# Two residual convolutions on one core: the work behind each of the last three 5x5 halves shared by three engines

## The chip, the cores and the metric

The kernel runs on one core of one Trainium2 chip. The metric is the device time of the core in microseconds (us), the median of three timed executions; a separate profiled execution gives the trace.

## The reference

`x` is 16 images of 32 channels, 128x128, float32. Two blocks follow each other, each with a group norm over 16 groups of two channels and a residual sum:

```python
x = x + conv3x3(gn(x), w3 * mask)      # padding 1; mask from a threshold on the mean |w3|
x = x + conv5x5(gn(x), w5) + bias      # written in the reference as a product of FFTs, padding 2
```

The 5x5 convolution is a circular convolution on a padded image, cut back to 128x128, so it equals a direct 5x5 convolution with padding 2.

## The kernel before

**Tiling.** An image is worked in two halves, so there are `HALVES` = 32 halves. The 128 partitions are four bands of 32 channels. TensorE multiplies 32x32 tiles of weights with 32 x 512 pieces of the image, sixteen of them for one tap (`tap`, L705), into four PSUM banks (`BANKS` = 4): banks 0 to 3 for the 3x3, banks 4 to 7 (`X5_BANK`) for the 5x5 convolution. The four banks of the 5x5 are used by every half anew; there is no second set.

**Precision.** Images and weights are split in a high and a low float16 part. A 5x5 half is three passes of 25 taps: the high image with the high weights, the high image with the low weights (both from the one tile `s5`, into which ScalarE copies `s5_hi` and `s5_lo` in turn, `weights5`, L363), and the low image `x5_lo` with `s5_hi` (`low_image`, L765). Tap 0 of the first two passes stands apart (`first5`, `last5`). The next half's first pass (`first5`) starts with `start=True` over the same banks, so it waits for `a5_go`, which ScalarE raises when it has evicted all four.

**Order.** The loop over steps `s` runs conv3x3 of half `s` and conv5x5 of half `s - LAG` with `LAG` = 3. Steps 3 to 31 mix both. In steps 32, 33 and 34 only the 5x5 convolution of halves 29, 30 and 31 is left: these are called lone steps here. There is no planner; the order on each engine is that of its program, and semaphores tie the engines together.

**Behind a half.** When `b5_whole` says that a half's matmuls are done, ScalarE evicts its four banks to `conv_out` (`take_conv5`, L350, activation at L355), GpSimd adds each to `mid` in place (`add_out`, L318, L322), and SP stores `mid` to the output with four DMAs of 256 KB, one for each band of partitions (L277), once all four additions are done. SP's program ends with waits on `out_stored` (L289). `mid` has five slots, `conv_out` one: an eviction of bank `b` waits for the addition of bank `b` of the half before.

**On VectorE.** In a step it computes the low image (`low5`, L574, L580), and for the next half the group statistics (`group_stats`, L526; `scale_of`, L541), the normalization (`normalize5`, L609, L557) and the clearing of padding rows (L565). ScalarE then makes the high image from it (`high5`, L343, L348). The order in a step is at L660 to L698 for VectorE and L382 to L426 for ScalarE; `low3` (L572) and `take_conv3` (L592) are its 3x3 work.

Of the kernel before, what the change touches and what calls it, by code (L numbers as in the profile page):

```python
# [48 lines left out]
def two_blocks(nc, x, w3_dram, thr_dram, w5_dram, bias_dram, mix_dram, out):  # L49
# [7 lines left out]
    with ExitStack() as ctx:  # L57
# [3 lines left out]
        def sem(name):  # L61
            return ctx.enter_context(nc.semaphore(name))
# [101 lines left out]
        var_ready = sem("var_ready")  # L164
        gstep = sem("gstep")
        out_added = sem("out_added")

        def has3(s):
            return 0 <= s < HALVES
# [11 lines left out]

        def exchange_number(s):
            return 1 if s == 2 else s // 2 + 1

        def column(kind):
            return slice(0, 1) if kind == "x" else slice(1, 2)
# [5 lines left out]
        def quad(q):  # L192
            return slice(q * C, (q + 1) * C)
# [16 lines left out]
        @block.sync  # L210
        def _(sp):
            def load_own(h):
                for j in range(Q):
                    sp.dma_start(x_own[quad(j), h % X_SLOTS, :, :], own_rows(x[h // 2], h % 2, j),
                                 ).then_inc(x_own_in[h % X_SLOTS], 16)

            def load_bands(h):
                for i in range(Q):
                    y0, y1, at = band(h % 2, i, 1)
                    sp.dma_start(x_bands[quad(i), h % XB_SLOTS, at:at + y1 - y0, :], x[h // 2][:, y0:y1, :],  # L220
                                 ).then_inc(x_bands_in[h % XB_SLOTS], 16)

            def move_rows(h, i, j, k, to, rows, at):

                sp.dma_start(mid_bands[quad(to), k % MB_SLOTS, at:at + rows.stop - rows.start, :],  # L225
                             mid[quad(j), h % MID_SLOTS, i, :].rearrange("p (a w) -> p a w", a=A)[:, rows, :],
                             ).then_inc(mid_bands_in[k % MB_SLOTS], 16)

            def move_mid(h):
                sp.wait_ge(mid_made, PIECES * (h + 1))  # L230
                for i in range(Q):
                    for j in range(Q):
                        move_rows(h, i, j, h, i, slice(0, A), 2 + A * j)

            def move_edges(n):

                for i in range(Q):
                    move_rows(2 * n + 1, i, 0, 2 * n, i, slice(0, 2), 2 + A * Q)
                    if i + 1 < Q:
                        move_rows(2 * n + 1, i, Q - 1, 2 * n, i + 1, slice(A - 2, A), 0)  # L240
                for i in range(Q):
                    move_rows(2 * n, i, Q - 1, 2 * n + 1, i, slice(A - 2, A), 0)
                    if i:
                        move_rows(2 * n, i, 0, 2 * n + 1, i - 1, slice(0, 2), 2 + A * Q)

            for q in range(Q):
                sp.dma_start(w3[quad(q), :, :], w3_dram.rearrange("i a b o -> i (a b) o")).then_inc(w3_loaded, 16)
            sp.dma_start(thr[:, :], thr_dram.rearrange("(a o) -> a o", a=1).to_broadcast([P, 1])).then_inc(w3_loaded, 16)
            load_bands(0)
            load_bands(1)  # L250
            sp.dma_start(mix[:, :], mix_dram).then_inc(mix_loaded, 16)
            load_bands(2)
            load_bands(3)
            load_own(0)
            for q in range(Q):
                sp.dma_start(w5[quad(q), :, :], w5_dram.rearrange("i a b o -> i (a b) o")).then_inc(w_loaded, 16)
                sp.dma_start(bias[quad(q), :], bias_dram.rearrange("(o a) -> o a", a=1)).then_inc(w_loaded, 16)
            load_own(1)
            load_bands(4)
            move_mid(0)  # L260
            load_own(2)
            move_mid(1)
            move_edges(0)
            load_bands(5)
            load_bands(6)
            load_own(3)
            move_mid(2)
            load_bands(7)
            load_own(4)
            load_bands(8)  # L270

            for s in range(LAG, STEPS + 1):
                if has5(s - 1):
                    k = s - 1 - LAG
                    sp.wait_ge(out_added, BANKS * (k + 1))
                    for j in range(Q):
                        sp.dma_start(own_rows(out[k // 2], k % 2, j), mid[quad(j), k % MID_SLOTS, :, :],  # L277
                                     ).then_inc(out_stored[k % MID_SLOTS], 16)
                if has3(s + XB_SLOTS):
                    sp.wait_ge(norm1, s + 2)  # L280
                    load_bands(s + XB_SLOTS)
                if has3(s):
                    move_mid(s)
                    if s % 2:
                        move_edges(s // 2)
                    if has3(s + X_SLOTS):
                        load_own(s + X_SLOTS)
            for n in range(MID_SLOTS):
                sp.wait_ge(out_stored[n], 16 * Q * len(range(n, HALVES, MID_SLOTS)))  # L289

        @block.gpsimd
        def _(pool):
# [24 lines left out]

            def add_out(k, b):  # L318

                pool.wait_ge(conv5_out, BANKS * k + b + 1)  # L320
                m = mid[:, k % MID_SLOTS, b, :]
                nc.gpsimd.tensor_tensor(m, m, conv_out[:, b, :], ALU.add).then_inc(out_added, 1)  # L322

            for k in range(HALVES):
                for b in range(BANKS):
                    add_out(k, b)

        @block.scalar
        def _(act):
# [20 lines left out]
            def take_conv5(k, b):  # L350

                act.wait_ge(b5_whole, k + 1)
                if k:
                    act.wait_ge(out_added, BANKS * (k - 1) + b + 1)
                nc.scalar.activation(conv_out[:, b, :], psum[:, X5_BANK + b, :], ACT.Identity,  # L355
                                     bias=bias[:, 0:1], scale=unscale[:, 1:2]).then_inc(conv5_out, 1)

# [24 lines left out]
            for s in range(STEPS + 1):  # L382
# [8 lines left out]
                if has3(s):  # L391
                    act.wait_ge(c3_inner, 3 * s + 1)
                    weights3(s3_lo, 1, 1)
                if has5(s - 1):
                    take_conv5(s - 1 - LAG, 2)
                    take_conv5(s - 1 - LAG, 3)
                if has5(s):
                    act.drain().then_inc(a5_go, 1)  # L398
                if has3(s):
# [5 lines left out]
                if has5(s):  # L405
                    if s == LAG:
                        act.wait_ge(w5_split, 3)
                    act.wait_ge(a5_inner, 2 * (s - LAG) + 1)
                    weights5(s5_lo)
                if gathered:  # L410
                    take_root(gathered[0])
                if s == 2:
# [16 lines left out]
        def _(dve):  # L429
# [179 lines left out]
            def normalize5(k):  # L609
# [3 lines left out]
                scalings += 1  # L613
                clear_pad(1, k, scalings)

            setup3()
            scalings = 0
            stats_in(0, range(BANKS))
# [41 lines left out]
            for s in range(LAG, STEPS):  # L660
                gathered = exchanged(s - 1)
                if s > HALVES:
                    dve.drain().then_inc(bank3_go, 1)
                low5(s - LAG)
                if has3(s):
                    low3(s)
                if s == LAG:
# [28 lines left out]
                    stats_in(s + 5, range(BANKS))  # L696
                if len(gathered) > 1:
                    scale_of(gathered[1])  # L698

        @block.tensor  # L700
        def _(pe):
# [212 lines left out]
```

## Time and profile before

| | |
|---|---|
| Timed executions | 880.46, 880.9 (median), 882.7 us |
| The profiled execution's own time | 882.4 us |
| Its span, first to last instruction | 880.6 us |
| TensorE matmul, busy | 789.2 us (90%) |
| VectorE, busy | 679.1 us (77%) |
| ScalarE, busy | 326.0 us (37%) |
| GpSimd, busy | 317.3 us (36%) |
| Mean granted TensorE clock | 0.964 |
| Chain that ended last | PE 77%, DVE 10%, issue 4%, SPq 3% |

[...] In a timeline, PE is TensorE's matmul, PEld its weight load, DVE VectorE, ACT ScalarE, POOL GpSimd; a letter q behind an engine is its queue (issues, waits and drains). What stands in square brackets is the idle time of the engine ahead of the row and what ended it. L711 is the line of the matmuls, L398 ScalarE's drain that raises `a5_go`.

### The profile page before, as it was taken

What the parts mean: (1) busy time and instruction counts of PE and PEld (TensorE: products, weight loads), DVE (VectorE), ACT (ScalarE), POOL (GpSimd) and SP (SyncE); (2) the same over time, 40 slices, a digit from 0 to 9 for tenths busy, and PEclk for the clock granted to TensorE, in tenths of its full rate; (3) what the DMA queues carried; (4) which work ended last, traced back from release to release, by engine and by line L of the source; (5) the groups of instructions that cost most, each with busy time, mean ns of one, the idle gap of its engine ahead of it and who ended that gap; (6) DMA issues with size and microseconds to landing.
All of it is one profiled execution on the core that took longest, in us unless ns stands there. A gap on an engine that the chain in (4) does not pass through costs nothing.

```text
span 880.6 us, 108990 instructions
## 1 busy us (share of the span) xinstructions
PE 789.2 (90%) x52300; PEld 705.5 (80%) x52300; DVE 679.1 (77%) x989; ACT 326.0 (37%) x417; POOL 317.3 (36%) x154
## 2 busy tenths in 40 slices
PE   1673579999999999999999999999999999998884
PEld 1552368888989889899888888988989889987773
DVE  5576378979898989989897989898998878664210
ACT  0122024344344444344434434444434443433331
POOL 1020004444433333334434444333334444443332
PEclk9887789999999999999999999999999999999998
DMA  8954965969787787868696868878795556454222
GB/s 178 211 120 116 221 153 135 234 144 225 172 215 201 198 207 188 218 168 223 151 236 144 221 178 206 211 196 208 182 220 157 158 147 160 107 136 114 66 56 56
DMA packets 83843, 150.52 MB, mean 171 GB/s; under 512 B 20960, under 2 KB 28384, under 8 KB 79712
## 3 DMA queue, kind: packets, MB, share of 16 engines
q1 hardware_dynamic: 79200, 145.92, 67.7%
q10 hardware_dynamic: 4608, 4.23, 1.9%
q14 instruction: 25, 0.20, 0.1%
q8 instruction: 10, 0.16, 0.1%
HBM read 75.60 MB, written 33.59 MB: 124 GB/s over the span
## 4 chain that ended last, share of the span: by engine, by line
PE 77%; DVE 10%; issue 4%; SPq 3%; DMA 2%; ACTq 1%; ACT 1%; DVEq 1%; POOL 0%; POOLq 0%
PE psum L711 76%; DVE x L572 3%; SPq L225 2%; DMA x_bands<-x_dram 2%; DVE bn_in L498 1%; DVE x_bands L557 1%; ACTq L398 1%; DVE bn_out L600 1%; DVE mid L592 1%; DVEq L595 1%; DVE mid_bands L557 1%; SPq L220 0%; DVE product L530 0%; POOL mid L322 0%; DVE deviation L534 0%
## 5 line engine op out<-in xcount | busy, mean ns | idle before, releaser
L322 POOL TENSOR_TENSOR mid<-mid,conv_out 128x512 f32<-128x512 f32 x128 | 308.0, 2437 | 502.4 <-ACT conv_out L355 489.1
L711 PE MATMUL psum<-x_hi,s 32*32 32x512 f16 x25600 | 378.0, 382 | 21.4 <-issue 9.7
L711 PEld LDWEIGHTS psum<-x_hi,s 32*32 32x32 f16 x25600 | 343.0, 88 | 47.3 <-issue 16.6
L711 PE MATMUL psum<-x,s 32*32 32x512 f16 x13824 | 228.9, 391 | 28.0 <-DVEq L595 14.7
L711 PEld LDWEIGHTS psum<-x,s 32*32 32x32 f16 x13824 | 176.4, 88 | 78.9 <-issue 49.2
L711 PE MATMUL psum<-x_lo,s_hi 32*32 32x512 f16 x12800 | 186.1, 376 | 3.5 <-issue 3.3
L711 PEld LDWEIGHTS psum<-x_lo,s_hi 32*32 32x32 f16 x12800 | 175.8, 88 | 8.4 <-issue 4.6
L580 DVE TENSOR_TENSOR x_lo<-mid_bands,x_hi 128x2560 f16<-128x2560 f32 x32 | 102.3, 3197 | 59.4 <-PE psum L711 59.0
L572 DVE TENSOR_TENSOR x<-x_bands,x 128x2304 f16<-128x2304 f32 x32 | 100.6, 3144 | 35.2 <-PE psum L711 35.2
L355 ACT ACTIVATE conv_out<-psum,bias,unscale 128x512 f32<-128x512 f32 x128 | 94.4, 769 | 60.1 <-PE psum L711 60.0
L364 ACT ACTIVATE s<-s_lo 128x800 f16<-128x800 f16 x32 | 27.9, 871 | 179.3 <-PE psum L711 179.3
L592 DVE SCALAR_TENSOR_TENSOR mid<-psum,unscale,x_own 128x1024 f32<-128x1024 f32 x64 | 79.1, 1277 | 8.1 <-PE psum L711 7.2
L341 ACT ACTIVATE x<-x_bands 128x2304 f16<-128x2304 f32 x32 | 67.9, 2122 | 45.8 <-DVE x_bands L565 22.9
L498 DVE BATCH_NORM_STATS2 bn_in<-x_bands 128x6 f32<-128x512 f32 x128 | 78.2, 673 | 3.2 <-DMA x_bands<-x_dram 3.1
L600 DVE BATCH_NORM_STATS2 bn_out<-mid 128x6 f32<-128x512 f32 x128 | 78.1, 668 | 2.3
L348 ACT ACTIVATE x_hi<-mid_bands 128x2560 f16<-128x2560 f32 x32 | 74.5, 2328 | 5.0 <-DVE mid_bands L565 5.0
L557 DVE TENSOR_SCALAR x_bands<-x_bands,gmean,gscale 128x2304 f32<-128x2304 f32 x32 | 71.2, 2226 | 0.1
L364 ACT ACTIVATE s<-s_hi 128x800 f16<-128x800 f16 x32 | 27.9, 872 | 113.6 <-PE psum L711 113.6
L557 DVE TENSOR_SCALAR mid_bands<-mid_bands,gmean,gscale 128x2560 f32<-128x2560 f32 x32 | 52.5, 1640 | 6.6 <-DMA mid_bands<-mid 4.5
L361 ACT ACTIVATE s<-s_lo 128x128 f16<-128x128 f16 x64 | 20.5, 321 | 40.5 <-PE psum L711 30.5
L334 ACT ACTIVATE root<-gvar 128x1 f32<-128x1 f32 x32 | 6.5, 202 | 71.6 <-DVE gvar L538 45.9
L530 DVE SCALAR_TENSOR_TENSOR product<-every_mv,mix 128x128 f32<-128x128 f32 x29 | 21.1, 726 | 15.4 <-DMA every_mv<-mv_scratch 15.0
(74 smaller groups left out, 175.1 us busy)
## 6 DMA issues: line engine op xcount, KB each, us to landing
x_own<-x_dram SPq DMA_DIRECT2D x128, 256.0 KB
mid_bands<-mid SPq DMA_DIRECT2D x512, 64.0 KB
out_dram<-mid SPq DMA_DIRECT2D x128, 256.0 KB
x_bands<-x_dram SPq DMA_DIRECT2D x96, 288.0 KB, 6.1
x_bands<-x_dram SPq DMA_DIRECT2D x32, 272.0 KB, 7.4
mid_bands<-mid SPq DMA_DIRECT2D x224, 32.0 KB
every_mv<-mv_scratch ACTq DMA_DIRECT2D x16, 256.0 KB
w<-L_conv_kernel_dram SPq DMA_DIRECT2D x4, 100.0 KB, 18.6
```

The source lines that it names most:

```text
L322: nc.gpsimd.tensor_tensor(m, m, conv_out[:, b, :], ALU.add).then_inc(out_added, 1)
L341: nc.scalar.activation(x3[:, :, 2:2 + W], x_bands[:, h % XB_SLOTS, :, :], ACT.Copy).then_inc(x3_go, 2)
L348: nc.scalar.activation(x5_hi[:, :, 2:2 + W], mid_bands[:, k % MB_SLOTS, :, :], ACT.Copy).then_inc(hi5_done, 1)
L355: nc.scalar.activation(conv_out[:, b, :], psum[:, X5_BANK + b, :], ACT.Identity, bias=bias[:, 0:1], scale=unscale[:, 1:2]).then_inc(conv5_ ...
L364: nc.scalar.activation(s5[:, :, :], source[:, :, :], ACT.Copy).then_inc(w5_go, 1)
L498: nc.vector.bn_stats(bn_in[:, h // 2 % 2, h % 2, b, :], rows.rearrange("p a w -> p (a w)")).then_inc(bn_x, 1)
L557: nc.vector.tensor_scalar(v, v, gmean[:, which:which + 1], gscale[:, which:which + 1], ALU.subtract, ALU.mult).then_inc(scaled, 1)
L572: nc.vector.tensor_tensor(at, x_bands[:, h % XB_SLOTS, :, :], at, ALU.subtract).then_inc(x3_go, 1)
L580: nc.vector.tensor_tensor(x5_lo[:, :, 2:2 + W], mid_bands[:, k % MB_SLOTS, :, :], x5_hi[:, :, 2:2 + W], ALU.subtract).then_inc(b5_go, 1)
L592: nc.vector.scalar_tensor_tensor(mid[:, h % MID_SLOTS, at, :], psum[:, X3_BANK + at.start:X3_BANK + at.stop, :], unscale[:, 0:1], x_own[:, ...
L600: nc.vector.bn_stats(bn_out[:, h % 2, b, :], mid[:, h % MID_SLOTS, b, :]).then_inc(bn_mid, 1)
L711: ins = nc.tensor.matmul(psum[quad(j), bank + i, :].rearrange("p (a w) -> p a w", a=A), w[quad(i), at, :], src[quad(i), A * j + dy:A * (j ...
```

## The change

Halves from `LATE` = 29 on are treated differently.

- **Eviction.** ScalarE evicts banks 0 and 1, VectorE banks 2 and 3 in one `tensor_scalar` instruction of 128x1024 (`take_late`). ScalarE waits for `late_out` before it raises `a5_go`.
- **Additions.** GpSimd adds banks 0 and 1, VectorE banks 2 and 3 in one `tensor_tensor` (`add_late`), for halves 29 and 30 in the next step behind the copy named below, for half 31 right behind its eviction.
- **Weight copy.** In steps 32, 33 and 34 the copy of `s5_lo` into `s5` is made by VectorE, behind `low5`. That of `s5_hi` stays with ScalarE.
- **Stores.** Each late half is stored in two groups of four DMAs of 128 KB: banks 2 and 3 when `late_added` has counted it, then banks 0 and 1 when GpSimd's two additions are counted.

`take_late(29)` and `take_late(30)` stand ahead of `low5` in steps 33 and 34. `added_before` gives the counts of evictions and additions, four for an early half and two for a late one.

```diff
--- before.py
+++ after.py
@@ -164,6 +164,8 @@
         var_ready = sem("var_ready")
         gstep = sem("gstep")
         out_added = sem("out_added")
+        late_out = sem("late_out")
+        late_added = sem("late_added")
 
         def has3(s):
             return 0 <= s < HALVES
@@ -181,6 +183,13 @@
 
         def exchange_number(s):
             return 1 if s == 2 else s // 2 + 1
+
+        LATE = HALVES - LAG
+        HALF_BANKS = BANKS // 2
+
+        def added_before(k, b):
+
+            return BANKS * min(k, LATE) + HALF_BANKS * max(k - LATE, 0) + b
 
         def column(kind):
             return slice(0, 1) if kind == "x" else slice(1, 2)
@@ -213,6 +222,11 @@
                 for j in range(Q):
                     sp.dma_start(x_own[quad(j), h % X_SLOTS, :, :], own_rows(x[h // 2], h % 2, j),
                                  ).then_inc(x_own_in[h % X_SLOTS], 16)
+
+            def store_out(k, banks):
+                for j in range(Q):
+                    sp.dma_start(own_rows(out[k // 2], k % 2, j)[:, banks, :], mid[quad(j), k % MID_SLOTS, banks, :],
+                                 ).then_inc(out_stored[k % MID_SLOTS], 16)
 
             def load_bands(h):
                 for i in range(Q):
@@ -272,10 +286,14 @@
             for s in range(LAG, STEPS + 1):
                 if has5(s - 1):
                     k = s - 1 - LAG
-                    sp.wait_ge(out_added, BANKS * (k + 1))
-                    for j in range(Q):
-                        sp.dma_start(own_rows(out[k // 2], k % 2, j), mid[quad(j), k % MID_SLOTS, :, :],
-                                     ).then_inc(out_stored[k % MID_SLOTS], 16)
+                    if k < LATE:
+                        sp.wait_ge(out_added, BANKS * (k + 1))
+                        store_out(k, slice(0, BANKS))
+                    else:
+                        sp.wait_ge(late_added, k - LATE + 1)
+                        store_out(k, slice(HALF_BANKS, BANKS))
+                        sp.wait_ge(out_added, added_before(k, HALF_BANKS))
+                        store_out(k, slice(0, HALF_BANKS))
                 if has3(s + XB_SLOTS):
                     sp.wait_ge(norm1, s + 2)
                     load_bands(s + XB_SLOTS)
@@ -286,7 +304,7 @@
                     if has3(s + X_SLOTS):
                         load_own(s + X_SLOTS)
             for n in range(MID_SLOTS):
-                sp.wait_ge(out_stored[n], 16 * Q * len(range(n, HALVES, MID_SLOTS)))
+                sp.wait_ge(out_stored[n], 16 * Q * sum(1 if k < LATE else 2 for k in range(n, HALVES, MID_SLOTS)))
 
         @block.gpsimd
         def _(pool):
@@ -317,12 +335,12 @@
 
             def add_out(k, b):
 
-                pool.wait_ge(conv5_out, BANKS * k + b + 1)
+                pool.wait_ge(conv5_out, added_before(k, b + 1))
                 m = mid[:, k % MID_SLOTS, b, :]
                 nc.gpsimd.tensor_tensor(m, m, conv_out[:, b, :], ALU.add).then_inc(out_added, 1)
 
             for k in range(HALVES):
-                for b in range(BANKS):
+                for b in range(BANKS if k < LATE else HALF_BANKS):
                     add_out(k, b)
 
         @block.scalar
@@ -351,7 +369,7 @@
 
                 act.wait_ge(b5_whole, k + 1)
                 if k:
-                    act.wait_ge(out_added, BANKS * (k - 1) + b + 1)
+                    act.wait_ge(out_added, added_before(k - 1, b + 1))
                 nc.scalar.activation(conv_out[:, b, :], psum[:, X5_BANK + b, :], ACT.Identity,
                                      bias=bias[:, 0:1], scale=unscale[:, 1:2]).then_inc(conv5_out, 1)
 
@@ -391,9 +409,11 @@
                 if has3(s):
                     act.wait_ge(c3_inner, 3 * s + 1)
                     weights3(s3_lo, 1, 1)
-                if has5(s - 1):
+                if has5(s - 1) and s - 1 < HALVES:
                     take_conv5(s - 1 - LAG, 2)
                     take_conv5(s - 1 - LAG, 3)
+                if s > HALVES:
+                    act.wait_ge(late_out, s - HALVES)
                 if has5(s):
                     act.drain().then_inc(a5_go, 1)
                 if has3(s):
@@ -405,8 +425,9 @@
                 if has5(s):
                     if s == LAG:
                         act.wait_ge(w5_split, 3)
-                    act.wait_ge(a5_inner, 2 * (s - LAG) + 1)
-                    weights5(s5_lo)
+                    if s < HALVES:
+                        act.wait_ge(a5_inner, 2 * (s - LAG) + 1)
+                        weights5(s5_lo)
                 if gathered:
                     take_root(gathered[0])
                 if s == 2:
@@ -612,6 +633,23 @@
                 normalize(1, k)
                 scalings += 1
                 clear_pad(1, k, scalings)
+
+            def take_late(k):
+
+                dve.wait_ge(b5_whole, k + 1)
+                if k == LATE:
+                    dve.wait_ge(out_added, BANKS * LATE)
+                else:
+                    dve.wait_ge(late_added, k - LATE)
+                at = slice(HALF_BANKS, BANKS)
+                nc.vector.tensor_scalar(conv_out[:, at, :], psum[:, X5_BANK + at.start:X5_BANK + at.stop, :],
+                                        unscale[:, 1:2], bias[:, 0:1], ALU.mult, ALU.add).then_inc(late_out, 1)
+
+            def add_late(k):
+
+                dve.wait_ge(late_out, k - LATE + 1)
+                m = mid[:, k % MID_SLOTS, HALF_BANKS:BANKS, :]
+                nc.vector.tensor_tensor(m, m, conv_out[:, HALF_BANKS:BANKS, :], ALU.add).then_inc(late_added, 1)
 
             setup3()
             scalings = 0
@@ -661,7 +699,13 @@
                 gathered = exchanged(s - 1)
                 if s > HALVES:
                     dve.drain().then_inc(bank3_go, 1)
+                    take_late(s - 1 - LAG)
                 low5(s - LAG)
+                if s >= HALVES:
+                    dve.wait_ge(a5_inner, 2 * (s - LAG) + 1)
+                    nc.vector.tensor_copy(s5[:, :, :], s5_lo[:, :, :]).then_inc(w5_go, 1)
+                if s > HALVES:
+                    add_late(s - 1 - LAG)
                 if has3(s):
                     low3(s)
                 if s == LAG:
@@ -696,6 +740,9 @@
                     stats_in(s + 5, range(BANKS))
                 if len(gathered) > 1:
                     scale_of(gathered[1])
+
+            take_late(HALVES - 1)
+            add_late(HALVES - 1)
 
         @block.tensor
         def _(pe):
```

## Rows read from the trace of the kernel before

**Rows 1.** Chain of waits that ended last, from 820 us: start us, us, what.
```profile
823.51 2.58 ACTq L398
...
826.13 7.41 PE psum L711 x393
...
833.56 0.88 ACT s L364
...
846.08 2.58 ACTq L398
...
868.02 0.79 ACT conv_out L355
...
868.88 2.48 POOL mid L322 x2
...
872.58 1.22 POOL mid L322
```
**Rows 2.** Timeline of TensorE, 802 to 870 us: start, duration, instruction, [idle before <- releaser].
```profile
826.13 7.38 PE L711 MATMUL psum<-x_hi,s 32*32 32x512 f16 x400 [2.94 <-ACTq L398]
834.49 5.79 PE L711 MATMUL psum<-x_hi,s 32*32 32x512 f16 x400 [0.98 <-ACT s L364]
...
848.70 6.99 PE L711 MATMUL psum<-x_hi,s 32*32 32x512 f16 x400 [2.93 <-ACTq L398]
```
**Rows 3.** Table by windows: length, busy (xcount) of PE, PEld, DVE, ACT, POOL; PEclk, DMA share, GB/s.
```profile
803.55:806.90 3.35, 3.35 (x128) 2.56 (x144) 0.09 (x2) 0.00 (x0) 3.35 (x3) 0.50 0.45 141
...
811.90:817.40 5.50, 5.50 (x400) 5.21 (x409) 2.68 (x7) 0.04 (x1) 0.00 (x0) 1.00 0.79 188
827.40:830.80 3.40, 3.40 (x155) 2.78 (x143) 1.53 (x2) 0.00 (x0) 3.40 (x2) 0.51 0.00 0
848.70:851.30 2.60, 2.60 (x112) 1.98 (x113) 0.05 (x1) 0.00 (x0) 2.60 (x3) 0.50 0.00 0
```
**Rows 4.** Groups by form, single lines and a stretch of the timeline: the durations of the operations.
```profile
L592 DVE SCALAR_TENSOR_TENSOR mid<-psum,unscale,x_own 128x1024 f32<-128x1024 f32 x64 | 79.1, 1277 | 8.1 <-PE psum L711 7.2
...
L465 DVE CAST s_hi<-w3n 128x256 f16<-128x256 f32 x1 | 0.3, 294 | 0.0
L467 DVE COPY s<-s_hi 128x128 f16<-128x128 f16 x1 | 0.2, 194 | 0.0
L470 DVE COPY s<-s_hi 128x160 f16<-128x160 f16 x1 | 0.2, 193 | 0.0
...
L355 ACT ACTIVATE conv_out<-psum,bias,unscale x16: 768/777/784, 800.7 to 870.0; 128x512 f32<-128x512 f32 x16
...
L364 ACT ACTIVATE s<-s_lo x3: 869/869/869, 811.0 to 855.7; 128x800 f16<-128x800 f16 x3
...
823.25 2.79 ACT L355 ACTIVATE conv_out<-psum,bias,unscale 128x512 f32<-128x512 f32 x4 [2.35 <-PE psum L711]
823.35 2.82 DVE L580 TENSOR_TENSOR x_lo<-mid_bands,x_hi 128x2560 f16<-128x2560 f32 x1 [8.42 <-PE psum L711]
```
**Rows 5.** Timeline of TensorE at its earlier holes, and the clock there by windows.
```profile
128.08 2.04 PE L711 MATMUL psum<-x_lo,s_hi 32*32 32x512 f16 x127 [1.71 <-issue]
131.72 1.52 PE L711 MATMUL psum<-x_lo,s_hi 32*32 32x512 f16 x90 [1.61 <-issue]
...
46.35 1.94 PE L711 MATMUL psum<-x,s 32*32 32x512 f16 x64 [2.10 <-DVEq L595]
...
46.20:49.20 3.00, 2.85 (x112) 2.27 (x124) 2.46 (x9) 0.51 (x2) 0.00 (x0) 0.50 0.27 66
126.30:128.10 1.80, 0.09 (x14) 0.02 (x7) 1.80 (x4) 0.67 (x1) 0.00 (x0) 1.00 0.30 73
130.20:131.70 1.50, 0.00 (x0) 0.00 (x0) 1.50 (x5) 0.00 (x0) 0.00 (x0) 1.00 0.35 83
```
**Rows 6.** Timeline of VectorE and ScalarE in the lone steps.
```profile
806.86 0.49 DVE L530 SCALAR_TENSOR_TENSOR product<-every_mv,mix 128x128 f32<-128x128 f32 x1 [3.26 <-DMA every_mv<-mv_scratch]
...
811.97 0.16 DVE L545 RECIPROCAL rinv<-root 128x1 f32<-128x1 f32 x1 [2.17 <-ACT root L334]
...
814.66 0.27 DVE L565 MEMSET mid_bands<- 32x256 f32 x1
...
841.15 2.32 ACT L348 ACTIVATE x_hi<-mid_bands 128x2560 f16<-128x2560 f32 x1
```
**Rows 7.** Timeline of GpSimd and VectorE, single instructions.
```profile
801.53 3.20 POOL L322 TENSOR_TENSOR mid<-mid,conv_out 128x512 f32<-128x512 f32 x1 [13.13 <-ACT conv_out L355]
804.69 1.27 POOL L322 TENSOR_TENSOR mid<-mid,conv_out 128x512 f32<-128x512 f32 x1
...
257.19 3.87 POOL L322 TENSOR_TENSOR mid<-mid,conv_out 128x512 f32<-128x512 f32 x1
...
259.85 3.63 DVE L572 TENSOR_TENSOR x<-x_bands,x 128x2304 f16<-128x2304 f32 x1
```
**Rows 8.** Timeline of SP's queue at single stores and one move, and the last transfer by window.
```profile
794.54 0.59 SPq L225 DMA_DIRECT2D mid_bands<-mid  x1
...
875.80 1.24 SPq L277 DMA_DIRECT2D out_dram<-mid  x1
...
874.90:879.90 5.00, 0.00 (x0) 0.00 (x0) 0.00 (x0) 0.00 (x0) 0.00 (x0) 0.50 0.87 210
```

## The prediction

> **What bounds the kernel now.** I read the chain of waits first, for the last 55 us, then the timeline of TensorE. The chain [rows 1] is TensorE's matmuls, broken in every lone 5x5 step (one with no 3x3 work) in two places and followed by a tail. The first break is 2.9 us: TensorE has finished a half (at 800.65, 823.23 and 845.80), four evictions run one after the other on ScalarE, and only the drain behind the last one lets the next half start (803.55, 826.13, 848.70). The second is 0.98 us, the copy of `s5_lo` into `s5` on ScalarE [rows 2]. In the tail the matmuls end at 868.0, GpSimd's fourth addition at 873.8, and the span 6.8 us later.
>
> The first break costs more than its length. [...] So the 400 matmuls behind the breaks take 7.38 and 6.99 us at 826.13 and 848.70, where an undisturbed pass takes 5.79 [rows 2]. Behind the 0.98 us break the clock stays at 1.00 [rows 3].
>
> **The first break.** Halves 29, 30 and 31 are late; half 28 is not, so the break at 800.65 stays whole. At the next two, ScalarE keeps banks 0 and 1, and VectorE takes banks 2 and 3 beside it in one 128x1024 instruction. ScalarE: an eviction takes 0.777 us and four take 2.79 [rows 4], a pitch of 0.67, so two take 1.45 and 1.35 us goes. VectorE: its first instruction behind the same release began 0.10 us after ScalarE's [rows 4]; the operation itself is not in the trace. It is bounded by 0.6 (twice as fast as the nearest) and 1.28; I take 1.28, since the 3x3 eviction L592 has the same shape, source and output type and one operand more [rows 4]. So it ends 1.38 us behind the release, a little before ScalarE's two. The added wait on `late_out` costs 0 to 0.2 us; I take 0.1. Behind it on ScalarE is queued the drain that releases TensorE. Each break shrinks by 1.25 us (bounds 1.0 to 1.35), two by 2.5, and 1.65 us of idle time stays in each.
>
> [...]
>
> **The clock behind the shorter break.** Does 1.65 us of idle time still let it fall? The nearest rows on one side are two holes of 1.71 and 1.61 us at 126 and 130 us, in which TensorE waited for nothing shown: the clock stayed at 1.00. On the other side a wait of 2.10 us ended at 46.35 and left the clock at 0.50 [rows 5]. I take "stays up". It returns 7.38-5.79 = 1.6 and 6.99-5.79 = 1.2 us, 2.8 together (bounds 0 and 2.8); I count 2.7.
>
> **The weight copies.** In the last three steps the copy of `s5_lo` moves to VectorE. ScalarE's takes 0.869 us [rows 4]. VectorE's float16 copies of 128 and 160 columns take 0.194 and 0.193 us, a cast of 256 from float32 0.294 [rows 4]. [...] I take 0.40. With VectorE's later start of 0.1 us the break goes from 0.98 to about 0.57: 0.4 us, 1.2 for three (bounds 0 to 1.6). VectorE is idle at those moments: its work ahead of them ends by 809.8, 829.0 and 848.8 [rows 6].
>
> That wait holds back what is queued on VectorE. In step 32 it is `group_stats`, `scale_of` and `normalize5(30)`, which ran from 806.86 to 814.93 [rows 6]. They start at about 811.3 and need 8.1 us less the 2.2 that they waited for the root behind ScalarE's copy, so they end near 817.4. `high5(30)`, which needs them, began at 818.57, behind ScalarE's other copy, and will want to begin at 818.2: hidden by 0.8 us, and by 3.1 until ScalarE is late for the next eviction (822.8, less 2.33 for `high5`); from there 1 us for each. In step 33 the copy and `add_late(29)` stand ahead of `normalize5(31)`, which moves from 826.10 to about 832 and ends by 834; its reader moves from 841.15 [rows 6] to 837.5. `low5` moves 1.3 us back and is wanted over 10 us later. All this at nothing.
>
> **Additions and stores.** In steps 33 and 34 VectorE adds behind the copy and SP stores later, in eight DMAs, with nothing else in SP's queue: nothing. Only the last half counts. ScalarE's first eviction frees GpSimd's first addition at 868.88, which ends at 870.14. VectorE's eviction ends at 869.4. Its addition then meets GpSimd's: an addition of 1.27 us took 3.20 when it started during VectorE's `low5`, and a `low3` begun at 259.85 took 3.63 us, of which the first 1.2 until GpSimd's addition ended at 261.06 [rows 7]. Each waits for the other's instruction. So VectorE's addition (1.15 by the shortest 128x1024 row, I take 1.2) runs from 870.1 to 871.3, and GpSimd's second to 872.5. SP's first store goes at 871.35 instead of 873.82. Stores of 256 KB were issued at a pitch near 0.65 us and moves of 64 KB take 0.59 [rows 8], so eight at 0.64: the last goes at 875.85, where it went at 875.80. Issue gains nothing; the transfer does. Four stores moved at 210 GB/s for 5.0 us, from 1.1 us behind the first issue, bound by transfer [rows 8]. Eight halves at 0.64 us ask for 205 GB/s and leave no backlog: the last lands at 875.85+1.1+0.65 = 877.6, and the span ends 0.7 us later, as before: 878.3, a gain of 2.3. I take 2.0, for the added wait between the groups. Bounds: 1.3, if the fourth store of each group holds SP for 1.24 us [rows 8], and 2.5, if the 1 MB simply starts 2.5 us earlier.
>
> [...]
>
> **Sum.** 2.5+2.7+1.2+2.0 = 8.4 us off the profiled execution, whose span is 880.6 and whose own time is 882.4, 1.5 over the median of the three runs, 880.9. The 1.8 us around the span stay. The executions differ by up to 2.2 us, about what one or two low stretches are worth, so the median may hold fewer of them than the profile; I don't correct for it. 880.9-8.4 = 872.5.
>
> **Rivals.**
> 1. The clock falls behind 1.65 us of idle time too. For it: the two holes are few, and 2.10 is not far. The 2.7 us stay away: 875.2.
> 2. VectorE at its upper bounds: copies as slow as ScalarE's, 880.9-7.2 = 873.7; or an eviction at twice its price, 2.6 us, which keeps both breaks and the falling clock, 880.9-3.2 = 877.7. Against both stand [rows 4].
> 3. A store costs by the piece, 5.0/4 = 1.25 us each whatever its size. Eight take 10 us from 872.5, the span ends at 883.2, a loss of 2.6 instead of a gain of 2.0: 877.1. Against it: 64 KB moves go out every 0.64 us without holding SP [rows 8].
> 4. Slower: VectorE's order turns against TensorE. The place is step 32, where the wait for `a5_inner` holds `normalize5(30)`. TensorE waits once `high5(30)` is 3.1 us late, 1 us for each; from 11.5 us on the kernel is slower, from 14 by over 0.3%; at 15 it is 884.4. Against it: the whole chain is 8.1 us, and nothing in it is new.
>
> **How the numbers follow.** Forecast 0.62; rival 1 0.21; rival 2 0.07, mostly the copies; rival 3 0.04; a mixture such as 2 with 3, under 0.3% (2.6 us, about what a measurement can tell here), 0.04; rival 4 0.02. The forecast's own bounds sum to 871.3 and 874.9. The range takes in half the spread of the runs below (870.5) and rival 1 with 1 us of its own bounds above (876.2). Faster 0.94, same 0.04, slower 0.02.
>
> **What would show it.** Right: behind halves 29 and 30 idle time near 1.65 us, and then 400 matmuls in 5.8 us at clock 1.00; three breaks near 0.57 at the copies; a VectorE eviction of 1.2 to 1.3 us; the first store 3.4 us behind the last matmul, eight issues with no long one among them, and the end 10.6 us behind the last matmul (12.6 before). Wrong: clock 0.50 behind the shorter breaks, a copy over 0.6 us, `late_added` behind both of GpSimd's additions, or a half of TensorE that starts behind `high5`.

## The result, and the profile after

The changed kernel takes 871.2 us (median of four executions, 868.44 to 875.01) where the kernel before takes 880.7 (878.21 to 882.7, four as well): a ratio of 0.9897, with a 95% interval of 0.9849 to 0.9944. Six more executions of the same kernel gave 869.6, beside eleven of the kernel before with 883.5: 0.9858 (0.9815 to 0.99). The forecast was 872.5. The profiled execution took 872.28 us, with a span of 870.5.

The executions of one kernel lie up to 9.6 us apart (876.96 to 886.55 for the kernel before in the second set), more than most parts of this change are worth. So the parts are read in a stretch that all traces share and that scatters little: the **lone stretch**, from half 28's first eviction to the end of the span. It is 880.6-800.67 = 79.9 us before and 870.5-801.35 = 69.15 after, 10.8 less. The **tail** within it runs from the last half's first eviction to the end of the span: 12.6 us before (from 868.02), 9.2 after (from 861.34).

The timeline of TensorE in the changed kernel, whose rows answer to [rows 2]: start, duration, instruction, and in brackets the idle time before it and what ended it.

```profile
804.22 7.16 PE L758 MATMUL psum<-x_hi,s 32*32 32x512 f16 x400 [2.91 <-ACTq L418]
811.84 5.79 PE L758 MATMUL psum<-x_hi,s 32*32 32x512 f16 x400 [0.47 <-DVE s L706]
...
824.73 5.72 PE L758 MATMUL psum<-x_hi,s 32*32 32x512 f16 x400 [1.59 <-ACTq L418]
...
843.80 5.73 PE L758 MATMUL psum<-x_hi,s 32*32 32x512 f16 x400 [1.59 <-ACTq L418]
850.00 5.78 PE L758 MATMUL psum<-x_hi,s 32*32 32x512 f16 x400 [0.47 <-DVE s L706]
```

The two late breaks are 1.59 us instead of 2.94 and 2.93, the 400 matmuls behind them take 5.72 and 5.73 us instead of 7.38 and 6.99, and the copy's breaks are 0.47 to 0.49 (three) instead of 0.98. The break behind half 28, which the change leaves alone, is still 2.91, with 7.16 us behind it. The table by windows (columns as in [rows 3]: the length of a stretch, how long each engine was busy in it, and under PEclk TensorE's granted clock as a part of full speed) shows the clock at 1.00 over the matmuls behind both breaks, where stretches of it were at 0.50 before, and at 1.00 in the second break itself (middle row):

```profile
824.73:830.50 5.77, 5.72 (x400) 5.24 (x400) 3.27 (x1) 0.00 (x0) 4.41 (x2) 1.00 0.00 0
842.25:843.80 1.55, 0.00 (x0) 0.00 (x0) 1.53 (x2) 1.45 (x2) 0.68 (x1) 1.00 0.00 0
843.80:849.53 5.73, 5.72 (x400) 5.19 (x400) 3.28 (x1) 0.00 (x0) 4.42 (x2) 1.00 0.00 0
```

The timeline of the new work on VectorE, with ScalarE and GpSimd beside it, in step 33 and behind the last matmul (the durations answer to [rows 4], the meeting of VectorE and GpSimd to [rows 7]):

```profile
823.19 1.44 ACT L373 ACTIVATE conv_out<-psum,bias,unscale 128x512 f32<-128x512 f32 x2 [2.35 <-PE psum L758]
823.20 1.34 DVE L645 TENSOR_SCALAR conv_out<-psum,unscale,bias 128x1024 f32<-128x1024 f32 x1 [6.52 <-PE psum L758]
...
830.51 0.37 DVE L706 COPY s<-s_lo 128x800 f16<-128x800 f16 x1 [2.51 <-PE psum L758]
830.79 1.22 DVE L652 TENSOR_TENSOR mid<-mid,conv_out 128x1024 f32<-128x1024 f32 x1
...
862.20 3.47 POOL L340 TENSOR_TENSOR mid<-mid,conv_out 128x512 f32<-128x512 f32 x2 [13.97 <-ACT conv_out L373]
862.72 1.82 DVE L652 TENSOR_TENSOR mid<-mid,conv_out 128x1024 f32<-128x1024 f32 x1
```

ScalarE's pair ends last, as the sum had it. VectorE's addition takes 1.22 us with GpSimd idle and 1.82 behind the last matmul, where GpSimd's first addition is under way.

The stores of the last half, single issues of SP (first, second and last of eight), and the transfer by window, whose rows answer to [rows 8]:

```profile
864.57 0.32 SPq L228 DMA_DIRECT2D out_dram<-mid  x1
864.93 0.43 SPq L228 DMA_DIRECT2D out_dram<-mid  x1
...
867.78 0.43 SPq L228 DMA_DIRECT2D out_dram<-mid  x1
...
865.40:869.50 4.10, 0.00 (x0) 0.00 (x0) 0.00 (x0) 0.00 (x0) 0.26 (x1) 0.50 0.92 253
```

An issue takes 0.43 us where the stores before took near 0.6 and the last of them 1.24, the pitch is 0.47, and 1 MB moves at 253 GB/s instead of 210. (The expectations below write 276 GB/s, which is 1.05 MB over 3.8 us; by windows such stores gave 244 to 253.)

### The profile page after: what moved, and what is told of

Same layout as the page of the kernel before. It is cut to its first block, busy times and chain, and to the rows that moved or that the text cites. A ratio compares the mean times of both kernels' runs of the same rounds, so it can differ in the third digit from the quotient of the medians.

```text
span 870.5 us, 108994 instructions
## 1 busy us (share of the span) xinstructions
PE 787.6 (90%) x52300; PEld 705.8 (81%) x52300; DVE 687.4 (79%) x998; ACT 319.6 (37%) x408; POOL 310.7 (36%) x148
## 4 chain that ended last, share of the span: by engine, by line
PE 78%; DVE 11%; issue 4%; SPq 3%; DMA 2%; DVEq 1%; ACT 1%; ACTq 0%; POOLq 0%; POOL 0%
PE psum L758 77%; DVE x L593 3%; SPq L239 2%; DMA x_bands<-x_dram 2%; DVE bn_in L519 1%; DVE x_bands L578 1%; DVE bn_out L621 1%; DVE mid L613 1%; DVEq L616 1%; DVE mid_bands L578 1%; SPq L234 1%; DVE product L551 0%; DVE gscale L570 0%; DVE x_lo L601 0%; DVE deviation L555 0%
## 5 line engine op out<-in xcount | busy, mean ns | idle before, releaser
L340 POOL TENSOR_TENSOR mid<-mid,conv_out 128x512 f32<-128x512 f32 x122 | 301.4, 2499 | 500.8 <-ACT conv_out L373 500.8
L373 ACT ACTIVATE conv_out<-psum,bias,unscale 128x512 f32<-128x512 f32 x122 | 90.3, 768 | 60.2 <-PE psum L758 60.1
L382 ACT ACTIVATE s<-s_lo 128x800 f16<-128x800 f16 x29 | 25.3, 871 | 157.8 <-PE psum L758 157.8
```

The source lines that it names most:

```text
L382: nc.scalar.activation(s5[:, :, :], source[:, :, :], ACT.Copy).then_inc(w5_go, 1)
```

## The experiments

Every kernel's lone stretch, its tail, and what followed the break behind half 28 (and behind 29 and 30), in the profiled executions. Most kernels have one such execution; the tail repeats within 0.1 us (9.1 or 9.2 in all five profiles with the changed kernel's last half: the changed kernel twice, both pauses, four late), so a single one can be read for it, while what follows a long break differs from one execution to the next.

| kernel | lone stretch | tail | breaks, and the 400 matmuls behind each |
|---|---|---|---|
| before | 79.9 | 12.6 | 2.91: 7.37; 2.94: 7.38; 2.93: 6.99 |
| changed | 69.15 | 9.2 | 2.91: 7.16; 1.59: 5.72; 1.59: 5.73 |
| changed, again | 67.6 | 9.1 | 2.91: 5.74; 1.59: 5.71; 1.59: 5.71 |
| copies only | 76.7 | 12.5 | 2.91: 5.78; 2.93: 5.72; 2.92: 8.60 |
| one group | 71.25 | 11.2 | 2.92: 7.24; 1.60: 5.71; 1.60: 5.72 |
| eight together | 70.3 | 10.3 | 2.94: 7.18; 1.60: 5.71; 1.59: 5.73 |
| by channels | 71.3 | 12.6 | 2.91: 5.78; 1.60: 5.72; 1.60: 5.72 |
| by bank | 76.3 | 17.6 | 2.93: 5.76; 1.60: 5.72; 1.60: 5.71 |
| pause a | 70.05 | 9.15 | 2.92: 5.71; 1.82: 5.71; 2.04: 7.39 |
| pause b | 72.6 | 9.1 | 2.95: 7.38; 2.35: 5.72; 2.67: 7.17 |
| GpSimd waits | 69.15 | 9.1 | 2.91: 7.19; 1.59: 5.72; 1.59: 5.72 |
| four late | 66.4 | 9.2 | 1.59: 5.75; 1.60: 5.72; 1.60: 5.73 |
| four late, fused | 64.6 | 7.2 | 1.57: 5.78; 1.59: 5.73; 1.60: 5.71 |
| the same, again | 64.5 | 7.2 | 1.64: 5.77; 1.59: 5.71; 1.60: 5.71 |

**The copies alone.** The kernel before with only this:

```diff
-                    act.wait_ge(a5_inner, 2 * (s - LAG) + 1)
-                    weights5(s5_lo)
+                    if s < HALVES:
+                        act.wait_ge(a5_inner, 2 * (s - LAG) + 1)
+                        weights5(s5_lo)
...
                 low5(s - LAG)
+                if s >= HALVES:
+                    dve.wait_ge(a5_inner, 2 * (s - LAG) + 1)
+                    nc.vector.tensor_copy(s5[:, :, :], s5_lo[:, :, :]).then_inc(w5_go, 1)
```

> The kernel before, with only the three copies of s5_lo in the last steps moved to VectorE. The lone stretch, from half 28's first eviction to the span's end, is 79.9 us in the kernel before and 69.15 in the changed one. Theory: each copy's break falls from 0.98 to 0.48 us, nothing else moves, the clock falls behind all three 2.9 us breaks as before: 78.4 us. Rival, that part of the gain behind the long breaks came from the shorter ones (the clock stays up once they are short): about 75.5, with the clock at 1.00 behind at least one 2.9 us break.

Measured: 76.7 us. The three copy breaks were 0.46, 0.48 and 0.47 us, so 1.5 us of the 3.2 is theirs. The rest is the clock. The theory that all three long breaks bring the clock down is wrong: they are as long as ever, but two of them left it up, which is the rival's sign, and the third cost more than any in the kernel before:

```profile
803.79 5.78 PE L715 MATMUL psum<-x_hi,s 32*32 32x512 f16 x400 [2.91 <-ACTq L398]
...
824.24 5.72 PE L715 MATMUL psum<-x_hi,s 32*32 32x512 f16 x400 [2.93 <-ACTq L398]
...
844.64 8.60 PE L715 MATMUL psum<-x_hi,s 32*32 32x512 f16 x400 [2.92 <-ACTq L398]
...
844.70:853.20 8.50, 8.50 (x400) 6.76 (x400) 0.00 (x0) 0.00 (x0) 4.79 (x4) 0.66 0.28 60
```

(The last row is the table by windows: a mean clock of 0.66 over those matmuls.) That gives 76.7 where the theory had 78.4 and the rival 75.5. So the length of 2.9 us alone does not decide whether the clock falls. The changed kernel shows the same behind half 28, where it is the kernel before in all that runs ahead of the break: 7.16 us in its first profile (above), and in its second

```profile
802.15 5.74 PE L758 MATMUL psum<-x_hi,s 32*32 32x512 f16 x400 [2.91 <-ACTq L418]
```

Over all kernels with a 2.9 us break behind half 28, 6 of 11 fell. What decides is not shown. Nor is the rival refuted for the breaks behind 29 and 30, the only ones with a copy break of the lone steps ahead of them: 2 of 2 fell with the long copies, 1 of 2 with the short ones, too few to tell.

**How long may a break be?** The changed kernel with a ScalarE copy of unused data ahead of the drain, of 1 and 3 rows of 128 columns in the one kernel and of 6 and 9 in the other:

```diff
+                if HALVES < s < STEPS:
+                    n = (1, 3)[s - HALVES - 1]          # (6, 9) in the second kernel
+                    nc.scalar.activation(x3[:, 0:n, 2:2 + W], x_bands[:, 0, 0:n, :], ACT.Copy)
                 if has5(s):
                     act.drain().then_inc(a5_go, 1)
```

> The changed kernel with a ScalarE copy of unused data (128 and 384 columns, about 0.25 and 0.5 us) ahead of the drain that starts the next half, in steps 33 and 34: breaks of about 1.8 and 2.05 us instead of 1.55. Theory, that the clock holds up to somewhere between 1.7 and 2.1 us: 1.00 behind the first, open behind the second; the lone stretch grows by 0.75 us (69.9), or by 2.2 where the second falls. Rival, that the clock held by luck at 1.55 us: 0.50 behind the first already, stretch 72 or more.

> As before it, with 768 and 1152 columns, about 0.8 and 1.1 us: breaks of about 2.4 and 2.7 us. Theory: the clock falls behind both, each costs the pause and 1.2 to 1.6 us of slow matmuls: stretch 69.15+1.9+2.8 = 73.9. Rival, that the fall in the kernel before came with the four evictions or GpSimd's work and not with the idle time: clock 1.00, stretch 71.1.

Measured, in the timeline of TensorE of each:

```profile
801.23 5.71 PE L761 MATMUL psum<-x_hi,s 32*32 32x512 f16 x400 [2.92 <-ACTq L421]
...
820.53 5.71 PE L761 MATMUL psum<-x_hi,s 32*32 32x512 f16 x400 [1.82 <-ACTq L421]
...
840.04 7.39 PE L761 MATMUL psum<-x_hi,s 32*32 32x512 f16 x400 [2.04 <-ACTq L421]
```

```profile
824.52 5.72 PE L761 MATMUL psum<-x_hi,s 32*32 32x512 f16 x400 [2.35 <-ACTq L421]
...
844.68 7.17 PE L761 MATMUL psum<-x_hi,s 32*32 32x512 f16 x400 [2.67 <-ACTq L421]
```

1.82 held, 2.04 fell, 2.35 held, 2.67 fell (by windows the clock over the 400 matmuls is 1.00, 0.77, 1.00 and 0.79): the theory that the clock falls behind both breaks of the second kernel is wrong, and one fixed length as the limit does not fit the three. Both rivals are wrong as well: the clock held at 1.82, and breaks of 2.04 and 2.67 us brought the slow matmuls back with only two evictions and two of GpSimd's additions beside them. Over all kernels, 15 breaks of 2.9 us ended with the clock down 9 times, and 23 of 23 breaks of 1.57 to 1.64 us left it up. (The lone stretches, 70.05 and 72.6 us, both lie 1.3 under what the theory had, 71.35 and 73.9: in the first kernel the clock also held behind half 28, in the second behind the break of 2.35.) So the idle time matters. Behind halves 29 and 30, in the kernels with the short copies, the clock fell behind 3 of the 5 breaks of 2.04 us and more, and behind none of the 20 near 1.6. At 2.9 us it falls in some executions and not in others; 2.04, 2.35 and 2.67 us were seen once each. The nine falls cost 1.24 to 2.85 us each over 5.75, together 14.7, so a 2.9 us break costs 1.0 us on average beyond its length, over these fifteen.

**One group of stores.** The changed kernel, with both waits ahead of four stores of 256 KB:

```diff
                         sp.wait_ge(late_added, k - LATE + 1)
-                        store_out(k, slice(HALF_BANKS, BANKS))
                         sp.wait_ge(out_added, added_before(k, HALF_BANKS))
-                        store_out(k, slice(0, HALF_BANKS))
+                        store_out(k, slice(0, BANKS))
```

> The changed kernel, but each late half is stored by four DMAs of 256 KB once both VectorE's and GpSimd's additions are done. Theory, that a store of 256 KB moves at 210 GB/s and that of 128 KB at 276: first issue 865.7-861.3 = 4.35 us behind the last matmul, span's end 6.8 us later, so 11.15 us of tail instead of 9.2 and a lone stretch of 71.1. Rival, that the faster transfer of the changed kernel was chance of that execution: the 1 MB takes 3.8 us here too, tail 10.2, stretch 70.2.

**Eight stores, all together.** Both waits stand ahead of the two groups, so nothing is stored before both additions are done.

> The changed kernel, but all eight DMAs of 128 KB are issued together, once both additions are done. Theory, that the smaller store is faster by itself (issue every 0.47 us, 276 GB/s): first issue 4.35 us behind the last matmul, end 5.95 later, tail 10.3. Rival, that the early start of the first group made the transfer faster: 210 GB/s or less, tail 11.1 or more.

**Eight stores by channels.** As the last, but 16 channels of four banks each:

```diff
-                        store_out(k, slice(HALF_BANKS, BANKS))
...
-                        store_out(k, slice(0, HALF_BANKS))
+                        for j in range(Q):
+                            for c0 in (0, C // 2):
+                                sp.dma_start(own_rows(out[k // 2], k % 2, j)[c0:c0 + C // 2, :, :],
+                                             mid[j * C + c0:j * C + c0 + C // 2, k % MID_SLOTS, :, :],
+                                             ).then_inc(out_stored[k % MID_SLOTS], 16)
```

> As the one with the eight stores together, but each DMA takes 16 channels of all four banks (8 KB in one piece for each partition, as in the kernel before) and not 32 channels of two banks. If the size of a DMA sets its speed: issue every 0.47 us, tail 10.3. If the shape does (8 KB for each partition, or 16 partitions): issue near 0.6 us, 210 GB/s, tail 11.1 or more.

**Four stores by bank.** One DMA for each bank, over all 128 partitions, banks 2 and 3 behind VectorE's addition, 0 and 1 each behind its own:

```diff
+            def store_bank(k, b):
+                to = out[k // 2].rearrange("c (i r j a) w -> r i j c (a w)", i=BANKS, r=2, j=Q)[k % 2, b]
+                sp.dma_start(to, mid[:, k % MID_SLOTS, b, :]).then_inc(out_stored[k % MID_SLOTS], 16)
```

> The changed kernel, but each late half is stored by four DMAs of 256 KB, each of one bank and all 128 partitions (2 KB for each partition). If what makes a store fast is a short piece for each partition: the transfer at 276 GB/s or more and a tail at or under 9.1 us. If it is the number of KB in a DMA: 210 GB/s, and 3.2+1.1+5.0+0.7 = 10.0 us.

The transfer of the last half by windows, for one group, eight together, by channels and by bank, in this order; the last two columns are the busy share of the 16 DMA engines and GB/s:

```profile
863.10:868.00 4.90, 0.00 (x0) 0.00 (x0) 0.00 (x0) 0.00 (x0) 0.00 (x0) 0.50 0.89 214
```

```profile
863.20:867.50 4.30, 0.00 (x0) 0.00 (x0) 0.00 (x0) 0.00 (x0) 0.00 (x0) 0.50 0.90 244
```

```profile
866.70:872.90 6.20, 0.00 (x0) 0.00 (x0) 0.00 (x0) 0.00 (x0) 0.00 (x0) 0.50 0.84 169
```

```profile
862.50:873.50 11.00, 0.00 (x0) 0.00 (x0) 0.00 (x0) 0.00 (x0) 0.00 (x0) 0.50 0.25 92
```

Single issues of SP: the fourth store of one group, the second of eight together, the first of eight by channels.

```profile
864.06 1.24 SPq L228 DMA_DIRECT2D out_dram<-mid  x1
```

```profile
862.88 0.43 SPq L228 DMA_DIRECT2D out_dram<-mid  x1
```

```profile
865.57 0.57 SPq L297 DMA_DIRECT2D out_dram<-mid  x1
```

One group gives a tail of 11.2 us and 214 GB/s, as the theory said. The fourth of its stores holds SP for 1.24 us again, at the same place as before. Eight together give 10.3 and 244 GB/s, as its theory said. So of the 2.0 us that the stores gain against one group, 0.9 comes from the shape of the stores and 1.1 from the earlier start. "Smaller is faster" is wrong, though: by channels the DMAs are 128 KB as well, are issued every 0.67 us and move at 169 GB/s, for a tail of 12.6. What counts is the shape, 4 KB from each of 32 partitions against 8 KB from each of 16; which of the two numbers does it, these runs don't tell. It isn't the size or the number of the packets: both kernels move the last half in 640 packets (512 of 2 KB, and 128 small ones).

By bank the theory fell altogether: a tail of 17.6 us. The mean busy share of the 16 DMA engines is 0.25 for the whole transfer, as much as four of them busy all the time would give (4/16). The small packets fall by the same factor: there are 16 for each DMA in the kernels above (64 for the four stores of one group, 128 for eight), and 16 for all four stores here, 4 for each. The outermost dimension of the target has four entries there, and 32 or 16 in all other stores. That this four is what keeps the share at 0.25 is the author's reading of one kernel; no run changes it alone.

**Taking turns.** GpSimd waits with the last half's two additions until VectorE has added:

```diff
+                if k == HALVES - 1:
+                    pool.wait_ge(late_added, HALVES - LATE)
                 pool.wait_ge(conv5_out, added_before(k, b + 1))
```

> The changed kernel, but GpSimd waits with its two additions of the last half until VectorE has added its two banks. Theory, that the two engines take turns at one port: VectorE's addition takes 1.22 us instead of 1.82 and ends 2.65 us behind the last matmul instead of 3.2; GpSimd's end 2.5 us later, at 5.2; the second group goes out after that, and the tail is 9.1 to 9.6 us. Rival, that VectorE's addition is 1.8 us here for another reason, such as the eviction right ahead of it: 1.82 again.

Measured, in the timeline:

```profile
857.24 1.22 DVE L654 TENSOR_TENSOR mid<-mid,conv_out 128x1024 f32<-128x1024 f32 x1
...
858.54 2.48 POOL L342 TENSOR_TENSOR mid<-mid,conv_out 128x512 f32<-128x512 f32 x2 [15.81 <-DVE mid L654]
```

1.22 us, with the same eviction right ahead of it: the 0.6 us more were GpSimd's. GpSimd's additions take 1.26 us each here, against 1.26 and 2.24 in the changed kernel. This shows that the two engines take turns; that it is at one port, as the theory has it, no run shows. The tail stays at 9.1, as the theory said. The first group goes out 0.6 us earlier, the second waits until 5.2 us behind the last matmul, and its four issues end where they did.

**Half 28 late as well.**

```diff
-        LATE = HALVES - LAG
+        LATE = HALVES - LAG - 1
...
-                if s > HALVES:
-                    act.wait_ge(late_out, s - HALVES)
+                if s >= HALVES:
+                    act.wait_ge(late_out, s - HALVES + 1)
```

On VectorE `take_late` and `add_late` start one step earlier, too.

> The changed kernel with half 28 treated as the late ones too, so the break behind it falls from 2.9 to 1.55 us. Theory: 1.35 us of idle time and 1.4 us of slow matmuls go, lone stretch 66.4, time about 2.8 us under the changed kernel's. Rival, that VectorE's addition ahead of the group statistics in step 32 makes the high image late: TensorE waits in step 33, up to 1 us.

The lone stretch is 66.4 us, as the theory said: the third break is 1.59 us, with 5.75 behind it. TensorE didn't wait for the high image. The 2.8 us that the theory wanted in the time did not show: it is 870.9 us (four executions, 868.33 to 872.98), 0.9878 of the kernel before (0.9822 to 0.9934), which can't be told from the changed kernel's.

**The last half finished by VectorE.** On top of that, the bias is added to `mid` in step 34, and the last half is done by two instructions, each followed by its four stores:

```diff
-            take_late(HALVES - 1)
-            add_late(HALVES - 1)
+            dve.wait_ge(biased, 1)
+            dve.wait_ge(b5_whole, HALVES)
+            for at in (slice(HALF_BANKS, BANKS), slice(0, HALF_BANKS)):
+                m = mid[:, (HALVES - 1) % MID_SLOTS, at, :]
+                nc.vector.scalar_tensor_tensor(m, psum[:, X5_BANK + at.start:X5_BANK + at.stop, :], unscale[:, 1:2], m,
+                                               ALU.mult, ALU.add).then_inc(late_added, 1)
```

> Half 28 late as well, and the last half finished by VectorE alone: the bias is added to mid ahead of time in step 34, and behind the last matmul two instructions of 128x1024 scale PSUM and add mid at once (1.28 us each, as the 3x3 eviction), each followed by its four stores. Theory: first store 1.35 us behind the last matmul, eight issues at 0.47, the last at 4.7, the end 2.7 later: tail 7.4 instead of 9.15, lone stretch 64.7; time 2.9+1.75 = 4.6 us under the changed kernel's. Rival, that the transfer and not the issue bounds the stores, once they start early: tail 7.9 or more.

> The kernel with four late halves and the last one finished by VectorE, once more. Its two profiles and that of its relative show 4 and 5 waits of 1.2 us of TensorE for the low image of the 3x3 convolution (where VectorE has met an addition of GpSimd), the changed kernel's show 0 to 4, though the work there is the same. Theory, that these are chance: 0 to 3 here, lone stretch 64.6 again, median 866 to 868. Rival, that the longer programs of the other engines bring them: 4 or more again, median near 869.

(The profiles that the last text speaks of are one of this kernel and one of the kernel with half 28 late.) The timeline of VectorE behind the last matmul:

```profile
860.77 2.48 DVE L756 SCALAR_TENSOR_TENSOR mid<-psum,unscale,mid 128x1024 f32<-128x1024 f32 x2 [9.14 <-PE psum L770]
```

Lone stretches of 64.6 and 64.5, a tail of 7.2 (from VectorE's first instruction): as the theory said. The time is not, which was to be 4.6 us under the changed kernel's. The medians are 868.8 (867.19 to 872.55) and 869.2 (864.87 to 871.04), six executions each, 0.9849 and 0.9847 of the kernel before (intervals of 0.981 to 0.9888 and 0.9814 to 0.9881). The changed kernel, run beside the first of them, had 869.6 and 0.9858 (the run expected here in these words):

> The changed kernel once more, for the price of the whole on more executions: 0.988 to 0.992 of the kernel before; behind the 2.9 us break of half 28 the clock may hold or fall, behind those of 1.55 us it holds; tail 9.15 us.

So 3 to 4.5 us less in the lone stretch show up as about 1 us in the median, inside the scatter. The rest is lost ahead of step 32: the lone stretch starts at 802.8 to 804.8 us in the three profiles with four late halves, at 795.85 to 802.5 in the eleven others. TensorE's waits between 150 and 795 us, in the kernel before and in the one with half 28 late (engine, line, what it waited for: us in total, times, longest):

```profile
PE psum L711 <- DVE x L572: 2.5, 2, 1.3
```

```profile
PE psum L759 <- DVE x L593: 6.0, 5, 1.2
```

A wait of 1.2 us comes where the low image of the 3x3 convolution meets an addition of GpSimd, as at 259.85 in [rows 7], behind which TensorE's next matmuls start at 263.54, after 1.22 us of waiting. There are 0 to 4 of them in the eleven profiles of the other kernels (2 in the changed kernel's first, none in its second) and 5, 4 and 3 in the three with four late halves. That the larger programs bring them is neither shown nor excluded: the last run had 3 of them, which both its theory and chance allow, and its median lies with the rival's. This stays open. The waits do account for much of the scatter in general: with their time taken off, the starts of the lone stretch lie between 795.5 and 799.3 in all fourteen profiles.

## Why the prediction held

**The first break: right, with its size.** 1.35 us went from each where 1.25 were counted. VectorE started 0.01 us behind ScalarE, not 0.10, and its eviction took 1.34 us, not 1.28: about the 1.38 that the sum had together. The wait on `late_out` cost nothing that can be seen, and the whole difference is the 0.1 counted for it. No row of the kernel before has this instruction; that of the 3x3 eviction, 1.28, was 0.06 us under it.

**The clock: right in the profiled execution, too large on average.** The clock stayed at 1.00 behind both, and 1.66 and 1.26 us came back, against 2.7 counted. But the step took the falls of the kernel before as certain, because all three had fallen in the one trace. Nine of fifteen do, at 1.0 us a break on average. By this average two breaks return 2.0 us, not 2.7; that the profile showed 2.9 is luck of the one trace before. The rule by which the shorter break was judged (1.7 holds, 2.1 falls) gave the right answer on too simple a ground: 2.35 held, and 2.04 fell, each once. Rival 1 did not occur in any of 23 breaks of this length.

**The copies: right, a little small.** The copy takes 0.37 us where 0.40 was taken. The 0.40, and the 1.6 us that the three breaks were to give at most, were the author's estimates: no row of the kernel before shows a copy of 800 columns on VectorE, and what the runs showed is 0.37 us and 1.5 us for the three. VectorE starts about 0.05 us behind the matmuls, as ScalarE did, not 0.1 later. The break is 0.47, not 0.57 (the sum's own terms, 0.98-0.87+0.40+0.10, give 0.61): 1.5 us for three, against 1.2; the run with the copies alone shows the same three breaks. In step 32 the held chain ended at 816.67, and `high5(30)` began at 818.51, behind ScalarE's own copy as before: hidden, as worked out.

**The stores: right in the mechanism, the term too small.** The tail lost 3.4 us against 2.0 counted. VectorE's addition met GpSimd's as foreseen, and the first store went 3.2 us behind the last matmul (3.4 counted). The step that failed is the pitch: "eight at 0.64 us" was taken from stores of 256 KB and moves of 64 KB, the halved stores went every 0.47, so the last was issued 1.34 us earlier behind the last matmul than the last of the four before (6.44 against 7.78) where the sum had no gain. Of the 3.4 us, 2.0 come from the stores (one group against the changed kernel: 11.2 to 9.2) and 1.4 from the evictions and additions ahead of them (12.6 to 11.2). Rival 3 has the sign wrong: the smaller stores move the same megabyte faster, in this shape (eight together 244 GB/s, one group 214).

**The sum.** 2.7 + 2.9 + 1.5 + 3.4 = 10.5 of the 10.8 us in the lone stretch; the other 0.2 to 0.3 is a shorter slow stretch behind half 28, which the change doesn't touch. The median fell by 9.5 us where 8.4 was forecast. The terms for the copies and the tail were 1.7 us too small together, the first break's 0.2, and the clock's, on average, 0.7 too large. So part of the agreement is luck: errors of both signs cancel, and in the second set of executions the ratio of 0.9858 makes 12.5 us.

## What to carry to other kernels

When TensorE waits for the emptying of its only PSUM banks, an idle engine that takes half of the evictions shortens the wait (here from 2.93 to 1.59 us) and may also keep the clock up (here behind 23 of 23 short breaks, against 6 of 15 long ones), and the second can be worth nearly as much as the first (2.0 us on average against 2.7 here). A slow stretch in one trace is one draw: count over several executions how often it occurs before it goes into a sum. Store a last result in pieces as it becomes ready, but look at what shape the DMA gets: the same megabyte moved at 253, 214, 169 and 92 GB/s here.

## What the runs showed of the hardware

- The clock behind 2.9 us of idle time fell in 9 of 15 cases, and one fall cost 2.85 us (the copies alone: 8.60 us for 400 matmuls at a mean clock of 0.66); behind 1.6 us in 0 of 23.
- A store of 2 banks by 32 partitions (128 KB) was issued in 0.32 to 0.44 us, one of 4 banks by 16 partitions (128 KB, by channels) in 0.57 to 0.75, the first three of 4 banks by 32 partitions (256 KB, one group and the kernel before) in 0.57 to 0.68; the fourth of the 256 KB stores in a row held SP for 1.24 us, none of eight of 128 KB did.
- Four DMAs whose target has an outermost dimension of four (by bank) kept the DMA engines busy at a mean share of 0.25, with four small packets each instead of 16, and moved at 92 GB/s.
- VectorE's two-input addition took 1.22 us alone (GpSimd waits) and 1.82 when GpSimd was under way (the changed kernel), GpSimd's 1.26 alone and 2.24 behind VectorE's: as if each waited for the other's instruction to end. Such meetings cost TensorE 1.2 us a time in the steady steps, 0 to 5 times for an execution, a good part of this kernel's scatter.
